# A macaron block of two expert layers around linear attention: the first rows of a phase are fetched at the end of the phase in front of it

## The reference

```python
x = x + 0.5 * ffn(layernorm(x))      # expert layer 1
x = x + attn(layernorm(x))           # linear attention over 4 x 2048 tokens, 16 heads
x = x + 0.5 * ffn(layernorm(x))      # expert layer 2, same weights

def ffn(x):                          # x: (T, D)
    top_v, top_i = top_k(x @ Wr, 2)
    p = softmax(top_v)
    # each expert takes its first 2560 tokens in order, the others are dropped
    h = silu(xe @ W1[e]) * (xe @ W3[e])
    y = h @ W2[e]
    out[token] += p * y              # for each of the token's two experts
```

## Time and profile before

| | |
|---|---|
| median of 3 executions | 3114.44 us (3113.65 to 3114.66) |
| the profiled execution | 3114.75 us |
| its span | 3112.9 us |
| PE busy | 2939.2 us, 94% of the span |
| DVE, ACT, POOL busy | 48%, 43%, 38% |
| mean granted TensorE clock | 0.955 of full speed |
| DMA | 198.59 MB, 64 GB/s over the span |

### The profile page before, as it was taken

The page is one execution under the profiler, slowest core; times in us unless marked ns, Lnnn a source line. Parts: engine busy times, 40 slices in busy tenths (PEclk is TensorE's granted clock), DMA queues, the critical chain, the costliest instruction groups (busy, mean ns, idle before and its releaser), DMA issues. The chain is left out here.

```text
span 3112.9 us, 58539 instructions
## 1 busy us (share of the span) xinstructions
PE 2939.2 (94%) x20826; PEld 2733.1 (88%) x20826; DVE 1485.5 (48%) x3647; ACT 1323.2 (43%) x2807; POOL 1179.8 (38%) x1566
## 2 busy tenths in 40 slices
PE   6769999999999999969999994999999999999997
PEld 5659999999999999968888884998999999999987
DVE  7833434343444434326777774434434343434432
ACT  4633434343444434324554553434434343434433
POOL 3853434434444434320211123443444443443432
PEclk6569999999999999989999996999999999999999
DMA  8443323232323232120112013423233222323211
GB/s 263 144 99 58 72 42 78 41 76 41 75 41 77 50 65 40 29 60 29 51 48 70 29 43 91 84 40 75 55 61 77 42 57 53 78 41 74 42 35 26
DMA packets 156455, 198.59 MB, mean 64 GB/s; under 512 B 15600, under 2 KB 128368, under 8 KB 156272
## 3 DMA queue, kind: packets, MB, share of 16 engines
q0 software_dynamic: 64128, 88.42, 17.7%
q1 hardware_dynamic: 81856, 97.30, 10.2%
q10 hardware_dynamic: 10288, 10.38, 1.0%
HBM read 115.93 MB, written 80.11 MB: 63 GB/s over the span
## 5 line engine op out<-in xcount | busy, mean ns | idle before, releaser
L1092 DVE TENSOR_TENSOR e_hid<-e_ps,e_gate 128x384 f32<-128x384 f32 (+1 forms) x640 | 382.0, 597 | 947.2 <-ACT e_gate L1053 912.2
L1095 DVE TENSOR_TENSOR e_h_lo<-e_hid,e_h_hi 128x384 fp32r<-128x384 f32 (+1 forms) x640 | 384.1, 600 | 399.2 <-ACT e_h_hi L1057 394.7
L1057 ACT ACTIVATE e_h_hi<-e_hid 128x384 fp32r<-128x384 f32 (+1 forms) x640 | 356.9, 558 | 409.0 <-DVE e_hid L1092 404.1
L1053 ACT ACTIVATE e_gate<-e_ps 128x384 f32<-128x384 f32 (+1 forms) x640 | 334.9, 523 | 352.6 <-PE e_ps L88 348.7
L86 PE MATMUL e_ps<-e_xT_hi,c_wa_hi 128*128 128x384 f32 (+1 forms) x1280 | 454.9, 355 | 14.5 <-DVE e_hid L1092 10.7
L86 PE MATMUL e_ps<-e_xT_hi,e_wb_hi 128*128 128x384 f32 (+1 forms) x1280 | 457.5, 357 | 0.8
L88 PE MATMUL e_ps<-e_xT_hi,e_wb_lo 128*128 128x384 f32 (+1 forms) x1280 | 457.7, 358 | 0.0
L87 PE MATMUL e_ps<-e_xT_lo,e_wb_hi 128*128 128x384 f32 (+1 forms) x1280 | 456.1, 356 | 0.0
L87 PE MATMUL e_ps<-e_xT_lo,c_wa_hi 128*128 128x384 f32 (+1 forms) x1280 | 451.7, 353 | 0.0
L88 PE MATMUL e_ps<-e_xT_hi,c_wa_lo 128*128 128x384 f32 (+1 forms) x1280 | 451.6, 353 | 0.0
L919 POOL DMA_INDIRECT e_xrow<-normed_rows,e_token x328 | 357.7, 1091 | 182.8 <-issue 143.3
(11 more groups left out here) (286 smaller groups left out, 5487.6 us busy)
## 6 DMA issues: line engine op xcount, KB each, us to landing
raw<-w SPq DMA_DIRECT2D x204, 256.0 KB
normed_rows<-r_xn SPq DMA_DIRECT2D x8, 1056.0 KB, 5.4
normed_rows<-mi_xn SPq DMA_DIRECT2D x8, 1056.0 KB, 4.8
r_xin<-x SPq DMA_DIRECT2D x8, 1024.0 KB, 8.1
x<-r_xin ACTq DMA_DIRECT2D x8, 1024.0 KB, 5.4
mi_x<-x SPq DMA_DIRECT2D x8, 1024.0 KB, 8.6
out<-mi_x SPq DMA_DIRECT2D x8, 1024.0 KB, 5.3
e_xrow<-normed_rows,e_token POOLq DMA_INDIRECT x328
```

The source lines that it names most:

```text
L1053: act.activation(gate[:, f % 2, 0:n], ps1[f % 2][:, 0:n], ACT.Silu).then_inc(gated, 1)
L1057: act.activation(h[0][:, f, 0:n], hid[:, f % 2, 0:n], ACT.Copy).then_inc(h_high, 1)
L1092: dve.tensor_tensor(hid[:, f % 2, 0:n], ps3[f % 2][:, 0:n], gate[:, f % 2, 0:n], ALU.mult).then_inc(hid_ready, 1)
L1095: dve.tensor_tensor(h[1][:, f, 0:n], hid[:, f % 2, 0:n], h[0][:, f, 0:n].bitcast(F32), ALU.subtract).then_inc(h_ready, 1)
```

## The change

At the end of route_phase and of middle_phase POOL waits for the stores of the normalized rows and for `slot_token` (`slots_ready`), and issues the first four gathers of the expert phase behind it into a new buffer, `ahead`, which stays allocated. PE's first `turn` of an expert phase reads that buffer. POOL's program in the expert phase stays as it was, with its own gather(0) (its weights are read from `xrow`). The expert phase's `gate` buffer now lies on the words of `ahead`. SP no longer waits for expert 1's raw weights at the end of route_phase.

At the end of e1_ SP waits until POOL has seen all adds landed (`all_added`, from an empty POOL instruction), and loads groups 0 to 2 of x1 into `raw`, which is now allocated for the whole program: group 0 in four pieces of 256 KB with a semaphore each, groups 1 and 2 whole. middle_phase reads its x1 ring there and doesn't load these groups; PE and DVE wait for each piece of group 0.

```diff
@@ Router
-        dve.tensor_tensor(token[:, 0:SCOLS], self.tokenf[:], self.unfilled[:], ALU.add)
+        dve.tensor_tensor(token[:, 0:SCOLS], self.tokenf[:], self.unfilled[:], ALU.add).then_inc(self.slots_ready, 1)
@@ new
+class Ahead:
+    def __init__(self, m):
+        self.words = m.sb("ahead", [P, BIG * DX])
+        self.xrow = self.words[:].rearrange("p (s d) -> p s d", s=BIG)
+        self.gate = self.words[:, 0:2 * BIG * P].rearrange("p (b t) -> p b t", b=2)
...
+    def gather(self, pool, xn, slot_token, phase):
+        for sub in range(BIG):
+            pool.indirect_dma_start(
+                self.xrow[:, sub, :], None, xn, bass.IndirectOffsetOnAxis(ap=slot_token[:, sub:sub + 1], axis=0),
+                bounds_check=ROWS - 1, oob_is_err=True).then_inc(self.rows_loaded[phase], 16)
+
+    def load_x1(self, sp, x1, x1_g):
+        for i in range(MG // 2):
+            sp.dma_start(x1[:, 0, 2 * i:2 * i + 2], x1_g[0][:, 2 * i:2 * i + 2]).then_inc(self.x_first[i], 16)
+        for g in (1, 2):
+            sp.dma_start(x1[:, g], x1_g[g]).then_inc(self.x_loaded[g], 16)
@@ route_phase, sync
                     sp.wait_ge(xn_stored[s], 16 * (GR // 2))
-                wait_raw(sp, raw_loaded, 1)
@@ route_phase, gpsimd
                                                ALU.subtract).then_inc(w_low, 1)
+                pool.wait_ge(cleared, 16 * 3)
+                for i in range(2):
+                    pool.wait_ge(xn_stored[i], 16 * (GR // 2))
+                pool.wait_ge(r.slots_ready, 1)
+                ahead.gather(pool, xn_out, slot_token, 0)
@@ expert_phase
-        gate = m.sb("gate", [P, 2, WIDE])
+        gate = ahead.gate
@@ expert_phase, sync
                 wait_raw(sp, raw_loaded, loaded + E - 2)
+                if phase == 0:
+                    sp.wait_ge(w_low, PIECES * (E + 1))
+                    sp.wait_ge(all_added, 1)
+                    ahead.load_x1(sp, rows_of(raw), groups_of(acc))
@@ expert_phase, gpsimd
                 wait_alone(pool, y_added, WORDS * n + WORDS + 16 * SMALL + 16, k.passed)
+                pool.nop().then_inc(all_added, 1)
                 wait_alone(pool, x_loaded, WORDS * n + WORDS, k.passed)
@@ expert_phase, tensor
-                turn(WORDS)
+                pe.wait_ge(ahead.rows_loaded[phase], WORDS)
+                turn(ahead.xrow)
@@ middle_phase
-        x1 = m.sb("x1", [P, 3, MG, D])
+        x1 = rows_of(raw)
...
+        def wait_x1(eng, g, c):
+
+            if g == 0:
+                if c % 2 == 0:
+                    eng.wait_ge(x_first[c // 2], 16)
+            elif c == 0:
+                eng.wait_ge(x_loaded[g % 3], 16 * (g // 3 + (g % 3 != 0)))
@@ middle_phase, sync
-                for g in range(3):
-                    load(g)
@@ middle_phase, gpsimd
                     r.pick_rows_singly(pool, g, g % 2)
+                for b in range(2):
+                    pool.wait_ge(xn2_stored[b], 16 * (MGS // 2))
+                pool.wait_ge(r.slots_ready, 1)
+                ahead.gather(pool, xn_out, slot_token, 1)
```

More of the change, by code:

```diff
@@ L667, in wait_raw, with route_phase @@
         eng.wait_ge(raw_loaded[q % 2], 16 * (PIECES // 2 * n + q // 2 + 1))
-def route_phase(nc, k, attention, x_in, xn_out, x1_out, out, slot_token, w, slot_a, raw, raw_loaded, tiles_out):
+def route_phase(nc, k, attention, x_in, xn_out, x1_out, out, slot_token, w, slot_a, raw, raw_loaded, ahead,
+                tiles_out):
     with ExitStack() as ctx:
@@ L828, in _, with expert_phase @@
                 r.tabulate(pe, GR - 1, False, True, 2)
-def expert_phase(nc, k, name, xn, acc, slot_token, w, slot_a, raw, raw_loaded, table, loaded):
+def expert_phase(nc, k, name, phase, xn, acc, slot_token, w, slot_a, raw, raw_loaded, ahead, table, loaded):
     with ExitStack() as ctx:
@@ L990, in _, with turn @@
                 pe.nop().then_inc(y_made, 1)
-                def turn(n_loaded):
-                    pe.wait_ge(x_loaded, n_loaded)
+                def turn(rows):
                     for half in range(KD):
@@ L996, in turn @@
                             ins = pe.transpose(psx[:, half, sub * P:(sub + 1) * P],
-                                               xrow[:, sub, half * P:(half + 1) * P], k.ident[:])
+                                               rows[:, sub, half * P:(half + 1) * P], k.ident[:])
                         ins.then_inc(x_turned, 1)
@@ L1020, in tile @@
                         ins.then_inc(h_made, 1)
-                    turn(WORDS * g + 2 * WORDS)
+                    pe.wait_ge(x_loaded, WORDS * g + 2 * WORDS)
+                    turn(xrow)
                     pe.wait_ge(y_kept, g + 2)
@@ L1105, in _, with rows_of, groups_of, middle_phase @@
                 experts(dve, tile)
-def middle_phase(nc, k, x1_in, xn_out, x2_out, slot_token, tiles_out):
+def rows_of(raw):
+    return raw[:].rearrange("p (b c d) -> p b c d", b=3, c=MG)
+def groups_of(t):
+    return t[0:T, :].rearrange("(g c p) d -> g p c d", p=P, c=MG)
+def middle_phase(nc, k, x1_in, xn_out, x2_out, slot_token, raw, ahead, tiles_out):
     with ExitStack() as ctx:
         m = Memory(nc, ctx, "mi_")
-        x1 = m.sb("x1", [P, 3, MG, D])
+        x1 = rows_of(raw)
         x2 = m.sb("x2", [P, 2, MG, D])
@@ L1136, in middle_phase @@
         tab = m.sb("tab", [P, SCOLS])
-        x_loaded = [m.sem(f"x_loaded{b}") for b in range(3)]
+        x_first, x_loaded = ahead.x_first, ahead.x_loaded
         n1_ready = m.sem("n1_ready")
@@ L1162, in middle_phase @@
         tab_kept = m.sem("tab_kept")
-        x1_g, x2_g, xn_g = (t[0:T, :].rearrange("(g c p) d -> g p c d", p=P, c=MG) for t in (x1_in, x2_out, xn_out))
+        x1_g, x2_g, xn_g = (groups_of(t) for t in (x1_in, x2_out, xn_out))
         STEPS = range(-2, NCH + TAB + 1)
@@ L1517, in macaron @@
         attention = dict(wqT=wqT, wkT=wkT, wvT=wvT, wcT=wcT, wc=wc, ltriT=ltriT, wr=wr)
[L1518 to L1525, removed]
+        raw = m.sb("raw", [P, WCOLS])
+        ahead = Ahead(m)
+        route_phase(nc, k, attention, x, xn, x1, out, slot_token, weights, slot_a, raw, raw_loaded, ahead, tiles[0])
+        expert_phase(nc, k, "e1_", 0, xn, x1, slot_token, weights, slot_a, raw, raw_loaded, ahead, tiles[0], 2)
+        middle_phase(nc, k, x1, xn, out, slot_token, raw, ahead, tiles[1])
+        expert_phase(nc, k, "e2_", 1, xn, out, slot_token, weights, slot_a, raw, raw_loaded, ahead, tiles[1], 2 + E)
 def kernel(L0_attn_X, L0_attn_Wq, L0_attn_Wk, L0_attn_Wv, L0_attn_Wc, L0_attn_Ltri,
```

11 lines of the change are left out of this document (7 added, 4 removed).

## The result

The changed kernel took 3121.8 us (median of 15 executions, 3115.9 to 3126.68) against 3114.66 us (15 executions, 3110.49 to 3118.6): ratio 1.0024, 95% interval 1.0018 to 1.0031. It is slower by 7.1 us, 0.24%, and the interval leaves out no change. The execution profiled had a span of 3122.0 us, so it is 9.1 us longer than the span before.

A forecast was written before the change was run, and what follows sets the result against it. PE was taken as the bound, busy 2939.2 of 3112.9 us, so only boundary losses could be won. +3.58 + 11.51 - 5.50 = +9.6 us on the profiled 3114.75, put at 3124.0 us against the median; range 3112.0 to 3128.0.

The forecast's parts named there:

- the barriers: Boundaries into e1_, into e2_ and into middle_phase: +3.58, +11.51 and -5.50 us, in sum +9.6 us.
- The Drain: POOL's Drain behind the gathers ahead: landing 1.94 plus 5.71 us, barriers into e1_ and e2_ 5.74 and 13.67 us later.
- the Drain waits for the landing only: Rival, both barriers into expert phases: Drain ends at the gathers' landing, barriers +0.03 and +7.96 us, 3112.6 us; chance 9%.
- POOL's chain as one piece, with 2.16 us of slack: Expert phase starts: POOL's work moves as a whole with the barrier; PE feels the delay less 2.16 us.
- PE's stall at turn(1) and the fallen clock: Expert phase starts: PE waits for gather(1), 7.9 us in e2_; slower clock adds nothing, or at most some 0.5 us each.
- x1 ahead: Boundary from e1_ to middle_phase: x1 loaded before the barrier lets ACT start its first xT 5.50 us sooner.
- The bound of 0: Boundary from e1_ to middle_phase: no gain if SP's Drain waits for the 3 MB of x1 loads.
- What an edit of the buffers costs: Expert phases: the shared gate buffer was said to add no wait; no term for moved addresses.
- The Drain of the boilerplate at 12 ns: Skill page figure for Drains on every engine, said to give the free Drain's time; POOL's 5.71 us rows disagreed.
- the rival of the free Drain: Both barriers into expert phases: Drain costs nothing, barriers -1.91 and +6.02 us, in all -5.7 us, 3108.7 us; chance 8%.

The follow-up runs named there:

- best1_gathers: The changed kernel with unused pads that set the distances of weights, xT and h, and expert 1's raw weights loaded at e1_'s start: 3096.28 us, ratio 0.9943.
- a_pad128: The changed kernel with one unused buffer of 128 bytes per partition in front of weight slot B: 3116.59 us, ratio 1.0003.
- b_pad128: The kernel before the change with one unused buffer of 128 bytes per partition in front of weight slot B: 3123.04 us, ratio 1.002.
- section 4: Two kernels on POOL's Drain, varying when gathers precede it and a fill behind them, against the changed kernel padded by 128 bytes or without gathers ahead: 3108.48 and 3110.54 us.

## Why the prediction came out, and where its steps were wrong

The time lies inside the range and on the side forecast, 2.2 us below 3124.0. That was luck: the barriers were to cost 9.6 us and gave -0.4, and a term that was missing, the addresses, brought the 7 us.

- **The Drain** is the step that failed: "I take landing at 1.94 us plus 5.71 us". It ended 3.4 and 2.0 us behind the last issue, not 7.65. It starts while the gathers are still being issued, and ends 0.20 to 0.22 us behind the last landing. What happened is the rival "the Drain waits for the landing only": the barrier was to come +0.03 and +7.96 us later there, and came +1.72 (9.91 less 8.19) and +8.09 later behind slot_token. The first is more because the landing beside the weight loads took longer, 3.17 us behind the last issue; in best1_gathers, where those loads are in e1_, it took 1.81. The rival had 9%, and 3112.6 us as its time; the barriers alone gave 3116.59 (a_pad128) against 3115.34.
- **POOL's chain as one piece, with 2.16 us of slack**: right. The row numbers handed over in tile 2's meta came 2.20 and 8.16 us later behind slot_token, step 2 -0.13 and +5.84, so the slack was 2.3 us at both.
- **PE's stall at turn(1) and the fallen clock**: 7.3 (216.8 less 209.5) and 7.9 us forecast, 8.96 and 9.08 measured, the turn at half clock. From the turn to step 2 it was 17.56 us instead of 14.97, less than the 3.5 us more that were forecast, and PE still waited 0.56 us for `hid` at its end, so nothing came on top: right.
- **x1 ahead**: -5.50 forecast for ACT's first xT; from e1_'s last matmul it came 17.76 instead of 23.14 us later, -5.38. The bound of 0, if SP's Drain waited for its loads, didn't come true.
- **What an edit of the buffers costs**: put at nothing without a reason. The `ahead` buffer was costed by its DMAs and by who waits for the gate; that it moves all that lies behind it in the partition was passed over, and that is +7.06 us by the stages and the whole measured difference, as b_pad128 and a_pad128 show from both sides.
- **The Drain of the boilerplate at 12 ns**: the Trainium skill's page "VectorE: DVE Perf Modes", section "The DRAIN you can't avoid", has about 12 ns on all five engines for the Drains of the preamble and postamble. The Drains here stand at the ends of the kernel's own blocks, so the page's figure gave no support to the rival of the free Drain, and no run here tests it. POOL's took 46 ns with no recent indirect DMA, 0.37 to 0.53 us in the two other cases of section 4, the time to the landing behind gathers in flight, and 5.7 us behind landed adds.

## What to carry to other kernels

Work put ahead of a barrier is only ahead for the engine that receives it; for the engine that issues it, everything behind the barrier is later, so ask first whose chain binds the second and third tile. An edit that adds or moves a buffer can change the distances between the operands of every matmul: compare start-to-start times of unchanged matmuls by form before an explanation is sought at the place of the edit, and try a pad of 128 bytes as a control. Such pads were worth more here (19 us with three of them) than the reordering between phases.

## What the runs showed that I had not expected

A matmul of fp32r operands (the type of the high and low halves here) at 512 columns took 227 ns from start to start where moving operand and weights lie a multiple of 256 bytes apart, and 229.6 to 235 ns at the other distances tried (32, 64, 96, 128 and 224 modulo 256), but for one part of three at 64, which took 226.6. At 256 columns with the operands' roles exchanged the middle part, L87, took 119.9 to 120.6 ns at distance 0, 118.1 to 119.3 at 96, 128 or 32, and 113.7 at 64. The Trainium skill's page "SBUF — State Buffer", section "SBUF: two separate sides", has contention between engines only at the port pair that DVE and GpSimd share, and has PE waiting for no other engine. That PE's time depends on where its own two operands lie is beside that rule, and no run here tells whether it is the two reads that meet. POOL's Drain behind gathers in flight ended 0.2 us behind their landing, and behind adds that had landed it took 5.7 us; a one-element fill behind landed gathers came with 0.53 us.
